# Latent projections and first attention of a two-layer network in one block, with a new order of the fetches of key rows

## What is computed

```python
c_q = x @ Wq_down                      # 512 -> 64
c_kv = x @ Wkv_down                    # 512 -> 64
q_c = (c_q @ Wq_up)                    # 128 heads of 4
q_r = (x @ Wq_rope)                    # 128 heads of 64
k_c = (c_kv @ Wk_up); v_c = (c_kv @ Wv_up)   # 128 heads of 4
k_r = x @ Wk_rope                      # 64, shared by the heads
scores = (q_c . k_c + q_r . k_r) / sqrt(68)
out = softmax(scores) @ v_c, then @ Wo
```

## Time and profile before

| what | value |
|---|---|
| median of 3 runs | 2581.71 us (2579.03 to 2586.39) |
| profiled execution, its own time | 2582.48 us |
| its span, first to last instruction | 2580.4 us |
| PE busy | 2475.7 us (96%) |
| DVE, ACT, POOL busy | 1559.7, 1391.2, 1131.6 us |
| mean granted clock of TensorE | 0.983 of full speed |

### The profile page before, as it was taken

How to read it: one execution, slowest core, us unless ns; L and a number is a source line. 1 busy time by engine, 2 the same in 40 slices (tenths; PEclk the granted TensorE clock), 3 DMA queues, 4 the chain that set the end, 5 groups by cost and what they waited for, 6 DMA issues and landing times. The chain is left out here.

```text
span 2580.4 us, 40504 instructions
## 1 busy us (share of the span) xinstructions
PE 2475.7 (96%) x12630; PEld 1862.1 (72%) x12630; DVE 1559.7 (60%) x2797; ACT 1391.2 (54%) x2147; POOL 1131.6 (44%) x1138
## 2 busy tenths in 40 slices
PE   6999999999999999999997899999999999999996
PEld 3677777777777777777775588777877887878774
DVE  5666666666666666666663523275756657557566
ACT  3577777777777777777776332242433324324232
POOL 0355565655555555655554133233334234334220
PEclk8899999999999999999999899999999999999998
DMA  5222222222222222222221322121001010010001
GB/s 193 49 44 53 50 52 44 54 45 52 52 44 52 52 52 44 52 46 52 52 44 44 117 88 86 37 82 41 16 24 41 0 41 16 24 41 16 1 1 53
DMA packets 47611, 125.38 MB, mean 49 GB/s; under 512 B 6033, under 2 KB 23441, under 8 KB 41426
## 3 DMA queue, kind: packets, MB, share of 16 engines
q1 hardware_dynamic: 47570, 124.85, 18.1%
HBM read 80.27 MB, written 10.49 MB: 35 GB/s over the span
## 5 line engine op out<-in xcount | busy, mean ns | idle before, releaser
L472 DVE TENSOR_REDUCE row_max<-ps_max 128x1 f32<-128x512 f32 x1024 | 670.3, 687 | 197.8 <-PE ps_max L539 175.2
L390 POOL TENSOR_TENSOR p_lo<-probs,p_hi 128x1024 f16<-128x1024 f32 x256 | 547.8, 2150 | 387.1 <-ACT p_hi L422 386.8
L417 ACT ACTIVATE probs<-ps_score 128x1024 f32<-128x1024 f32 x512 | 523.6, 1023 | 251.1 <-PE ps_score L554 227.8
L552 PE MATMUL ps_score<-Q,K 128*128 128x512 f32 x1024 | 406.5, 397 | 2.1 <-ACT probs L417 2.1
L554 PE MATMUL ps_score<-Q,K 97*128 97x512 f32 x1024 | 406.1, 397 | 0.0
L539 PE MATMUL ps_max<-KX,Q 68*128 68x512 f32 x1024 | 379.6, 412 | 13.0 <-DMA KX<-content_k 7.6
L466 DVE TENSOR_TENSOR Q<-ps_x,Q 64x512 fp32r<-64x512 f32 x256 | 176.4, 689 | 247.6 <-ACT Q L412 243.9
L422 ACT ACTIVATE p_hi<-probs 128x1024 f16<-128x1024 f32 x256 | 269.5, 1053 | 4.1
L539 PEld LDWEIGHTS ps_max<-KX,Q 68*128 68x128 f32 x1024 | 189.3, 190 | 89.4 <-issue 37.8
L552 PEld LDWEIGHTS ps_score<-Q,K 128*128 128x128 f32 x1024 | 194.1, 190 | 60.7 <-ACT probs L417 11.1
L554 PEld LDWEIGHTS ps_score<-Q,K 97*128 97x128 f32 x1024 | 194.7, 190 | 38.4
(11 more groups left out here) (242 smaller groups left out, 4451.5 us busy)
## 6 DMA issues: line engine op xcount, KB each, us to landing
Q<-Q SPq DMA_DIRECT2D x64, 512.0 KB, 4.3
ffn_raw<-in_w_ffn SPq DMA_DIRECT2D x22, 768.0 KB, 4.3
w_raw<-in_w_qrope SPq DMA_DIRECT2D x32, 512.0 KB, 3.7
wq_raw<-in_wq SPq DMA_DIRECT2D x8, 1024.0 KB, 5.5
wo_raw<-in_wo SPq DMA_DIRECT2D x8, 1024.0 KB, 4.8
Q<-content_q SPq DMA_DIRECT2D x64, 64.0 KB
K<-content_k SPq DMA_DIRECT2D x64, 64.0 KB
wkv_raw<-in_wkv SPq DMA_DIRECT2D x8, 512.0 KB, 3.6
```

The costliest lines, as they stand in the source:

```text
L390: pool.tensor_tensor(p_lo[:, j, :, :], probs[:, j, 0:PAIRED, :], p_hi[:, j, :, :], ALU.subtract)\
L417: act.activation(probs[:, j, 2 * half:2 * half + 2, :], ps_score[half][:, :, :], ACT.Exp, scale=SCALE).then_inc(exped, 1)
L472: dve.tensor_reduce(row_max[:, t, j:j + 1], ps_max[t % 2][:, :], axis=AXX, op=ALU.max)\
L552: pe.matmul(ps_score[half][:, k, :], K1[:, b, t * P:(t + 1) * P], Q1[:, b, j, :], start=True, stop=False)
```

## The change

`latent_stage` is gone. Its jobs stand in `mla_stage`, ahead of the first group, in the same block. Its tiles lie in buffers of the attention that are not yet in use (`probs`, `p_parts`, `V`, `oT`), its banks are those of the scores, maxima, queries and outputs. The stores of the content rows have a semaphore for each part m, and the fetches for group 0 wait for part 0 alone. The r job of batch 1 and the eight v jobs are issued between the first maxima. The two pairs of first queries go to two banks. Zeroing and ones of batch 1 and the low part of the first weights go from DVE to POOL; the low rope keys are computed once and copied to the other three heads by POOL instead of computed four times by DVE. In all steps the fetch of `KX` stands behind the send of the row of maxima, one step earlier than before, m00 waits for `KX` and one row of `Q2` (`max_in`), and the scores for the other rows (`content_in`). ACT's wait for the first weights and the two copies into `w_hi` (lines 429 to 431) are unchanged, but the jobs now follow them in ACT's program. The later norm stages share one set of semaphores over their four rounds. The core of the diff (of `latent_stage`, all lines are removed):

```diff
+        def bank(n):
+
+            k = n % 8 if n < N_R else n % 4
+            if k < 4:
+                return ps_score[k // 2][:, k % 2, :]
+            return (ps_max[0], ps_max[1], ps_x, ps_o)[k - 4][:, :]
...
+            def rows(tile, src, g, b, row, parts, landed):
+                at = ROPE + row * HD0
+                sp.dma_start(tile[at:at + parts * HD0, b, :, :].bitcast(F32),
+                             dram[src][bass.ds(g * GH, GH), 0:parts * HD0, b * S:(b + 1) * S].rearrange("h r t -> r h t"))\
+                  .then_inc(landed, 16)
+
+            def max_keys(g, b):
+                rows(KX, "content_k", g, b, 0, 1, max_in[b])
+
             def content(g, b):
-
-                for tile, src, row, parts in ((Q2, "content_q", 0, 1), (Q2, "content_q", 1, 2),
-                                              (K2, "content_k", 0, 2), (K2, "content_k", 2, 1),
-                                              (KX, "content_k", 0, 1)):
-                    rows = dram[src][bass.ds(g * GH, GH), 0:parts * HD0, b * S:(b + 1) * S].rearrange("h r t -> r h t")
-                    at = ROPE + row * HD0
-                    sp.dma_start(tile[at:at + parts * HD0, b, :, :].bitcast(F32), rows).then_inc(content_in[b], 16)
+                rows(Q2, "content_q", g, b, 0, 1, max_in[b])
+                rows(Q2, "content_q", g, b, 1, 2, content_in[b])
+                rows(K2, "content_k", g, b, 0, 2, content_in[b])
+                rows(K2, "content_k", g, b, 2, 1, content_in[b])
...
             load_w(0)
...
+            def store(m):
+                for i, k in enumerate("qk"):
+                    n = NB + 2 * NB * m + NB * i + NB - 1
+                    sp.wait_ge(job_high, n + 1)
+                    sp.wait_ge(job_low, n + 1 - NB)
...
+            store(0)
+            store(1)
+            sp.wait_ge(parts_out[0], 64)
+            sp.wait_ge(zeros_set, 2)
+            sp.wait_ge(rows_set, 4)
+            for b in range(NB):
+                max_keys(0, b)
+                content(0, b)
+            store(2)
+            store(3)
+            sp.wait_ge(parts_out[1], 64)
             copy_q(0, 0)
+            for m in range(2, DC):
+                sp.wait_ge(parts_out[m], 64)
...
                     sp.dma_start(Q2[MROW:MROW + 1, b, :, :].bitcast(F32), mrow[0:GH, :].bitcast(F32)).then_inc(row_in, 16)
+                    if not last:
+                        max_keys(g + 1, b)
                     if b == 0 and not last:
...
+            for tile in (Q2, K2):
+                pool.tensor_copy(tile[ROPE:P, 1, :, :], zeros[ROPE:P, :].rearrange("p (a s) -> p a s", a=1)
+                                 .broadcast_to([ROPE, GH, S])).then_inc(rows_set, 1)
+            pool.wait_ge(rows_set, 2)
+            pool.wait_ge(zeros_set, 2)
+            for b in range(NB):
+                pool.tensor_copy(K2[MROW:MROW + 1, b, :, :], ones[MROW:MROW + 1, :].rearrange("p (a s) -> p a s", a=1)
+                                 .broadcast_to([1, GH, S])).then_inc(rows_set, 1)
+            pool.wait_ge(rows_set, 4)
+            for pair in range(2):
+                pool.wait_ge(w_step, pair + 1)
+                pool.tensor_tensor(w_lo[:, :, pair, :], w_raw[:, :, pair, :], w_hi[:, :, pair, :],
+                                   ALU.subtract).then_inc(w_split, 1)
+            for b in range(NB):
+                pool.wait_ge(rope_low, b + 1)
+                pool.tensor_copy(K2[0:ROPE, b, 1:GH, :], K2[0:ROPE, b, 0:1, :].broadcast_to([ROPE, GH - 1, S]))\
+                    .then_inc(rope_spread, 1)
...
+                act.activation(out, bank(n), ACT.Copy).then_inc(job_high, 1)
+                if kind == "r":
+                    act.wait_ge(job_high, n + 1)
+                    for j in range(GH):
+                        act.activation(KX[0:ROPE, b, j, :], K1[0:ROPE, b, :], ACT.Copy).then_inc(rope_set, 1)
+
+            for n in range(N_R):
+                job(n)
+            job(N_R)
+            high(0, 0, 0)
+            high(0, 0, 1, ps_o)
+            job(N_R + 1)
+            for n in range(N_V, N_V + 6):
+                job(n)
+            act.wait_ge(job_made, len(jobs))
+            for n in range(N_V + 6, len(jobs)):
+                job(n)
+            for m in range(DC):
+                act.wait_ge(parts_out[m], 64)
...
+            def rope_keys(b):
+                n = N_R + b
+                dve.wait_ge(job_high, n + 1)
+                dve.tensor_tensor(K2[0:ROPE, b, 0, :], bank(n)[0:ROPE, :], K1[0:ROPE, b, :], ALU.subtract)\
+                   .then_inc(rope_low, 1)
...
+            rope_keys(0)
             for pair in range(2):
-                dve.wait_ge(w_step, pair + 1)
-                dve.tensor_tensor(w_lo[:, :, pair, :], w_raw[:, :, pair, :], w_hi[:, :, pair, :],
-                                  ALU.subtract).then_inc(w_split, 1)
-            for pair in range(2):
-                low(0, 0, pair)
+                dve.wait_ge(parts_out[pair], 64)
+                low(0, 0, pair, (ps_x, ps_o)[pair])
                 for j in range(2 * pair, 2 * pair + 2):
                     for t in range(ST):
                         take_max(0, j, t)
+                if pair == 0:
+                    rope_keys(1)
+            for m in range(2, DC):
+                dve.wait_ge(parts_out[m], 64)
...
-                    pe.wait_ge(content_in[b], 80 * (g + 1))
+                    pe.wait_ge(max_in[b], 32 * (g + 1))
...
+                    pe.wait_ge(content_in[b], 48 * (g + 1))
...
+                if kind == "r":
+                    if parts[0] == 0:
+                        pe.wait_ge(krope_in, 16)
+                    for c in range(2 * parts[0], 2 * parts[-1] + 2):
+                        last = pe.matmul(out, w_krope[:, c, :], xT[:, c, b * S:(b + 1) * S], start=c == 0, stop=c == DC - 1)
+                    if parts[-1] == 0:
+                        return
...
+            pe.wait_ge(up_in, 32)
+            pe.wait_ge(job_high, NB)
+            for n in range(NB, N_R):
+                job(n)
+            job(N_R)
+            pe.wait_ge(x_split, 2 * DC)
             for pair in range(2):
-                if pair:
-                    pe.wait_ge(q_low, 1)
+                pe.wait_ge(job_high, N_R - 4 + pair + 1)
+                pe.wait_ge(job_low, N_R - 4 + pair + 1 - NB)
                 for third in range(3):
-                    queries(0, 0, pair, third)
-            for j in range(GH):
-                for t in range(ST):
-                    max_scores(0, 0, 0, j, t, wait_free=4 * j + t >= 2)
+                    queries(0, 0, pair, third, (ps_x, ps_o)[pair])
+            pe.wait_ge(rope_set, GH)
+
+            def first_max(k):
+                max_scores(0, 0, 0, k // 4, k % 4, wait_free=k >= 2)
+
+            first_max(0)
+            first_max(1)
+            job(N_R + 1, (0,))
+            first_max(2)
+            first_max(3)
+            job(N_R + 1, (1,))
+            first_max(4)
+            first_max(5)
+            for t in range(TT):
+                if t < 5:
+                    first_max(6 + 2 * t)
+                    first_max(7 + 2 * t)
+                job(N_V + t)
+            pe.wait_ge(set_up, 8)
...
+                        if first and b == 0 and (kind, at) == ("m", [0, 0]):
+                            pe.wait_ge(job_high, len(jobs))
+                            pe.wait_ge(rope_set, NB * GH)
+                            pe.wait_ge(rope_spread, NB)
```

More of the change, by code:

```diff
@@ L36 @@
 EXP_SHIFT = 8 * math.log(2.0)
[L39 to L132, removed]
-                    for j in range(GH):
[L134 to L187, removed]
-                if n >= 8:
-                    pe.wait_ge(act_done, n - 7)
-                    if n - 8 >= NB and jobs[n - 8][0] != "v":
-                        pe.wait_ge(dve_done, n - 7 - NB)
-                out = bank[n % 8][:, :]
-                if kind == "r":
-                    if b == 0:
-                        pe.wait_ge(krope_in, 16)
-                    for c in range(DC):
-                        last = pe.matmul(out, w_krope[:, c, :], xT[:, c, b * S:(b + 1) * S], start=c == 0, stop=c == DC - 1)
-                else:
-                    if n == NB:
-                        pe.wait_ge(up_in, 32)
-                        pe.wait_ge(act_done, NB)
-                    if kind == "q":
-                        last = pe.matmul(out, w_up[0:LAT, m * P:(m + 1) * P], cT[0:LAT, b * S:(b + 1) * S],
-                                         start=True, stop=True)
-                    elif kind == "k":
-                        last = pe.matmul(out, w_up[LAT:P, m * P:(m + 1) * P], cT[LAT:P, b * S:(b + 1) * S],
-                                         start=True, stop=True)
-                    else:
-                        last = pe.matmul(out, cT[LAT:P, m * P:(m + 1) * P], w_up[LAT:P, D:2 * D],
-                                         start=True, stop=True)
-                last.then_inc(ps_full, 1)
@@ L254, in mla_stage @@
```

(21 more changed lines are left out.)

173 lines of the change are left out of this document (132 added, 41 removed).

## The result

The changed kernel takes 2559.23 us (median of four runs, 2558.39 to 2563.6) beside 2580.62 us for the kernel before: a ratio of 0.9917, with a 95% interval of 0.9897 to 0.9936. That is 21.4 us faster where 34 were forecast, inside the range of 2541 to 2564, and 11 us above the number. The profiled execution took 2563.6 us, with a span of 2561.8; it is the slowest of the four, 4 us above their median, so that not all that its trace shows need hold for the other three. From the page of the changed kernel: the busy time by engine and the group of the maxima's matmuls (was line 539).

A forecast was written before the change was run, and what follows sets the result against it. PE, busy for 96% of the span, was taken as the bound, with gaps in prologue and steps. 2582.5 − 23.7 (prologue) − 1.0 (step 0) − 10 (steps) = 2547.8, said as 2548 us; 8-in-10 range 2541 to 2564.

The forecast's parts named there:

- the case that I held to be mine: Whole kernel: the forecast of 2548 us with no rival coming true, range 2541 to 2556, chance 0.43.
- T of step 0: End of prologue: forecast 56.5 us, 23.7 earlier than 80.17; expected sign 53 to 60, wrong if later than 60.
- rival 1: Prologue: the low clock stays through the first maxima, costing 12 us and 1 to 2 in the jobs; 2561 us, chance 0.17.
- the steps: 61 steady steps: m00 no longer waits for the late `KX` fetch; gain 10 us, bounds 5 and 12.
- The added wait: Each step, ahead of the first score: one more PE wait, at most 0.03 us each, 1.9 in all, probably hidden.
- rival 2: Steps: the `Q2` row or row of maxima becomes late instead of `KX`; the 10 us stay away; 2558 us, chance 0.10.
- rival 5: Steps: `KX`, sent right behind the row of maxima, slows it and delays every score start; 2616 us, chance 0.03.
- The weights' wait on ScalarE: Prologue start: ACT waits for the weights before copying the latents; cost 2.3 us, bounds 0 and 4.5.
- "nothing" for the fills: Prologue: zero and row fills moved to POOL take 9.8 us, are covered by 9 us and cost nothing.
- The rival's price of 3.5 us: Prologue: POOL's fills and DVE's splits exclude each other, moving T by 3.5 us; 2551 us, chance 0.10.
- the first maximum: Prologue: its rows, fetched behind the stores, land at 34 to 37 us; 36.2 taken for the first maximum.
- Now PE has fillers: Prologue, stretch of first maxima: argument that filler jobs between the maxima speak against the clock staying low.

The follow-up runs named there:

- experiment 1: Kernel before with only the steps' new fetch order (keys of the maxima behind the row of maxima, two semaphores of waits): 2569.48 us, ratio 0.9948 to the kernel before.
- experiment 2: Changed kernel with the keys of the maxima fetched last again, behind the four content rows, in all steps: 2570.2 us, ratio 0.9960 to the kernel before.
- experiment 6: Changed kernel with GpSimd's four fills held back until VectorE has split xT: 2557.43 us, ratio 0.9902 to the kernel before.
- experiment 8: Changed kernel with the content rows of batch 0, group 0, fetched ahead of the stores of part 1: 2555.55 us, ratio 0.9887 to the kernel before.
- experiment 9: Changed kernel with 128-row value jobs, latent copies first, fills held back, and batch 0's rows fetched ahead of part 1's stores: 2546.28 us, ratio 0.9849.
- experiment 4: Changed kernel with extra thrown-away matmuls, 8 ahead of the first maximum and 6 ahead of the ninth: 2549.46 us, ratio 0.9886 to the kernel before.
- experiment 3: Changed kernel with the whole rope key job of batch 1 moved ahead of the first maximum: 2559.32 us, ratio 0.9916 to the kernel before.
- experiment 5: Changed kernel with its eight value jobs over all 128 rows instead of 64, zeros in the others: 2550.91 us, ratio 0.9866 to the kernel before.

## Why the prediction was right or wrong

The time came out inside the stated range, but not by the case that I held to be mine. T of step 0 at 68.8 us lies far outside "between 53 and 60", and "later than 60" was my own sign of being wrong. What happened is in the main rival 1, given 0.17. The range held because it had been widened to take that rival in, and because the steps gave what was forecast.

**Right: the steps.** 10 us were forecast and 10.2 came, from the wait that was named; experiments 1 and 2 show it from both sides. The added wait costs nothing that can be seen, and rivals 2 and 5, a new wait in the steps, did not come: PE has no idle time in 1256 us.

**Right: the shape of the prologue to 38 us.** The weights' wait on ScalarE cost 1.1 us instead of 2.3 (latents at 17.12 instead of 16.02): they landed at 15.0, near the lower bound. Queries began within 0.4 us of the forecast.

**Wrong: "nothing" for the fills.** Their cover was read against the time at which the weights are needed, not against what they do to VectorE. They took 10.2 us of GpSimd, and VectorE's four casts and four subtractions took 15.8 us instead of 7.7, until 21.3. I had taken the small effect at 1.88 us as the price and put the rule of the Trainium skill, page "SBUF — State Buffer", section "SBUF: two separate sides", by which one of the two engines shuts the other out for a whole instruction, into a rival. The trace agrees with the rule: with the overlap taken away the durations are 0.69 and 1.22 again, where they were 2.38 and 2.79 (experiment 6). The last cast and subtraction, 1.75 and 2.18 us, stood beside GpSimd's subtractions for the low weights (from 16.50 on), which had moved to GpSimd too. PE lost 1.08 us in the middle of the content jobs. What all this cost the kernel's time is less than the runs can tell (experiment 6). The rival's price of 3.5 us was too high: VectorE began 2.3 us after ScalarE's first content copy (19.0), and queries started only 0.4 us later than forecast.

**Mis-sized: the first maximum.** 38.57 instead of 36.2. The term that was too small is the landing: the fetches were put behind the stores' issue, to land at 34 to 37, but the maximum was released by the `Q2` row at 38.5, 7 us after the first fetch was issued (31.34). Experiment 8 took 2.0 us of that away.

**Wrong: the clock in the stretch of maxima.** This is the term that carries the miss. "Now PE has fillers" was my reason against rival 1, priced at 12 us and given 0.17. The fillers kept PE busy, and that was not enough. The 19.3 us from the first maximum to T were right for a clock of 1.00 (19.4 in experiment 9, 20.5 with some 1.4 us added in experiment 4); the error was to take that clock. Measured were 10.9 us more between the first maximum and T than forecast, and 4.0 us more in step 0 (23.68 where 19.7 was expected). The sum closes: 0.4 for the queries' start, 1.9 for the row beyond that, 10.0 for the rest to T (10.9, less the 1 us that I had added for the clock), 4.0 in step 0, less 0.2 in the steps and some 0.3 elsewhere, is the 15.8 us between 2547.8 and 2563.6. Of these some 4 us belong to the profiled execution alone, which is that much above the median. Step 0 may be where: it took 23.68 us here and 19.9 in the three traces in which its clock did not fall (experiments 2, 3 and 6), close to the 19.7 expected. What should have warned me is the trace of before behind the prologue's idle stretch: PE's queries and maxima ran from 58 to 82 us, with PE busy for 20.3 of the 24, and from 58 on the clock was back only from 64.8 to 68.2 before T.

What brings the clock down exactly is not settled. Experiments 3 and 8 exclude the one wait ahead of the first maximum as the cause of the long fall; in experiment 4, with more dense matmuls in the stretch, it did not come; in experiment 5 the clock came back while matmuls with full rows ran. A wait of PE alone does not decide: the same 1.33 us was followed by a fall in experiment 5 and by none in 9 and 10. Whether it is the number of rows in use or something that goes with it is open too. The other runs of each kernel have no profile, so that how often the clock falls in them is open; the spread of the changed kernel's four runs, 5 us, and of experiment 4's, 12 us, fits a clock that does not always fall at the same place.

## What to carry to other kernels

A wait that ends by a transfer in the same microsecond as the work beside it costs a little in every step, and a fetch whose buffer is long free should be asked for when the buffer becomes free: 0.17 us in each of 61 steps was half of what this change won. When the serial start of a kernel is folded into its first stage, ask of each filler not only how long it takes but which clock it leaves: matmuls with few rows can fill TensorE and still leave it at half speed, and zero rows that cost no time may win it back. Fills moved from VectorE to GpSimd lengthen VectorE's work while it copies between buffers; look at both engines' durations before calling them free.

## What was not expected of the hardware

- TensorE, busy without a pause from 54 to 65 us with matmuls of 64 and 68 rows, stayed at a granted clock of 0.50; with 128 rows in the value jobs it went back to 1.00 while they ran, and eight records took 3.9 us instead of 7.2 (experiment 5).
- Two value records and two maxima took 1.72 us a turn with value jobs of 64 rows and 1.32 with 128, both at full clock (experiments 4 and 9).
- A kernel with 3.2 us more work on TensorE ran 8 to 10 us faster, in three of its four runs (experiment 4).
- VectorE's subtraction of 128x1024 took 2.79 us beside GpSimd's fill and 1.22 without, its cast 2.38 and 0.69; GpSimd's fill in turn took 2.80 beside VectorE and 1.89 alone.
